# An adaLN, recurrence and FFN kernel on one Trainium2 core: the rows of six projection blocks turned by transposing DMAs instead of TensorE

## What is computed

```
x  = x + attn(cond(x, cond_512))          # first half
#   cond: modulated 512x512 product, demodulated and clipped
#   attn: h = rmsnorm; gates, a linear recurrence over the tokens;
#         hs2 = out * gate + residual
#         h2 = rmsnorm(hs2); p = (h2 @ fc) * gelu(h2 @ gate)   # 1536 wide
#         result = p @ out_w.T + out_b + hs2                  # the projection
x  = x + ffn(cond2(x, ids, states))       # second half
#   cond2: layer norms with gathered gains, a 3072 -> 512 -> 512 network
#   ffn: int8 quantisation by rows, a 512x512 product, scales
```

## Time and profile before

| what | us |
|---|---|
| median of 3 runs | 1764.82 |
| lowest and highest | 1763.02, 1766.92 |
| the profiled execution, its own time | 1766.26 |
| span of the profile | 1764.4 |
| TensorE (PE) busy | 1744.7 |
| its weight loads (PEld, beside PE) | 1419.6 |
| VectorE (DVE) busy | 1184.4 |
| ScalarE (ACT) busy | 892.9 |
| GpSimd (POOL) busy | 786.7 |

### The profile page before, as it was taken

How to read it: one execution, slowest core, us unless ns; L and a number is a source line. 1 busy time by engine, 2 the same in 40 slices (tenths; PEclk the granted TensorE clock), 3 DMA queues, 4 the chain that set the end, 5 groups by cost and what they waited for, 6 DMA issues and landing times.

```text
span 1764.4 us, 23639 instructions
## 1 busy us (share of the span) xinstructions
PE 1744.7 (99%) x8047; PEld 1419.6 (80%) x8047; DVE 1184.4 (67%) x1753; ACT 892.9 (51%) x1329; POOL 786.7 (45%) x702
## 2 busy tenths in 40 slices
PE   9999999999899999999999999999999999999998
PEld 7888888888788888888888888776887888888886
DVE  8756667569989687795563344437976577577555
ACT  7655555555676575764652222334554443544533
POOL 1111221122766656674550000016577877778742
PEclk9999999999999999999999999999999999999999
DMA  6011110120343233233536666985645444534401
GB/s 206 1 48 48 48 48 0 48 72 24 120 133 129 101 122 138 96 105 122 192 105 220 196 233 215 337 284 181 226 135 172 146 138 148 164 124 151 148 23 61
DMA packets 105800, 229.72 MB, mean 130 GB/s; under 512 B 9906, under 2 KB 10162, under 8 KB 105700
## 3 DMA queue, kind: packets, MB, share of 16 engines
q1 hardware_dynamic: 75540, 152.97, 25.3%
q0 software_dynamic: 11776, 41.95, 7.1%
q10 hardware_dynamic: 18384, 33.56, 5.7%
HBM read 169.73 MB, written 58.72 MB: 129 GB/s over the span
## 4 chain that ended last, share of the span: by engine, by line
PE 87%; DVE 5%; DMA 2%; issue 2%; ACT 1%; SPq 1%; POOL 1%; DVEq 0%; ACTq 0%
PE bank L1058 25%; PE bank L348 17%; PE bank L2025 13%; PE bank L1121 12%; PE bank L2049 5%; PE bank L2070 5%; PE bank L328 4%; PE bank L1991 2%; PE bank L2000 2%; DMA x1T_d<-x_columns 1%; SPq L1918 1%; DMA x_columns<-xT 1%; POOL u L613 1%; PE bank L1131 1%; DVE h_parts L1470 1%
## 5 line engine op out<-in xcount | busy, mean ns | idle before, releaser
L1058 PE MATMUL bank<-h_parts,mlp_w 128*128 128x512 f32 x2016 | 460.1, 389 | 4.5 <-DVE mlp_w L1474 2.4
L1058 PEld LDWEIGHTS bank<-h_parts,mlp_w 128*128 128x128 f32 x2016 | 378.0, 188 | 85.3 <-DVE mlp_w L1474 2.8
L348 PE MATMUL bank<-h_parts,gate_w 128*128 128x512 f32 x1536 | 351.1, 389 | 0.6 <-DVE h_parts L681 0.6
L348 PEld LDWEIGHTS bank<-h_parts,gate_w 128*128 128x128 f32 x1536 | 288.2, 188 | 61.8 <-issue 0.9
L2025 PE MATMUL bank<-operand_parts,int_w 128*128 128x512 f32 x1152 | 281.8, 394 | 0.4 <-DVE x_columns L1572 0.4
L1121 PE MATMUL bank<-p_parts,mlp_out_w 128*128 128x512 f32 x1152 | 275.2, 396 | 6.1 <-DVE p_parts L1484 6.1
L1121 PEld LDWEIGHTS bank<-p_parts,mlp_out_w 128*128 128x128 f32 x1152 | 215.1, 189 | 56.5 <-issue 11.8
L2025 PEld LDWEIGHTS bank<-operand_parts,int_w 128*128 128x128 f32 x1152 | 213.1, 188 | 44.4 <-PE bank L1121 0.8
L1390 POOL TENSOR_TENSOR product_out<-product_out,gelu 128x512 f32<-128x512 f32 x72 | 125.3, 1761 | 97.4 <-DVE product_out L1542 96.8
L608 POOL TENSOR_TENSOR decay_sq<-decay 128x512 f32<-128x512 f32 x32 | 39.2, 1226 | 278.8 <-DVE decay L694 278.8
L1270 ACT ACTIVATE product_copy<-bank,vec_sb 128x512 f32<-128x512 f32 x144 | 99.0, 688 | 106.7 <-PE bank L1058 105.8
(11 more groups left out here) (308 smaller groups left out, 2809.0 us busy)
## 6 DMA issues: line engine op xcount, KB each, us to landing
p_d<-product_out SPq DMA_DIRECT2D x96, 256.0 KB, 2.0
p_tile<-p_d ACTq DMA_DIRECT2D x96, 256.0 KB, 4.8
raw_mlp_w<-mlp_gate_g SPq DMA_DIRECT2D x21, 512.0 KB, 3.6
raw_mlp_w<-mlp_fc_g SPq DMA_DIRECT2D x21, 512.0 KB, 4.4
xin<-xT SPq DMA_DIRECT2D x8, 1024.0 KB
hs_d<-u SPq DMA_DIRECT2D x8, 1024.0 KB, 5.0
hs_pair<-hs_d SPq DMA_DIRECT2D x8, 1024.0 KB, 7.7
x_columns<-xT SPq DMA_DIRECT2D x8, 1024.0 KB, 6.8
```

The costliest lines, as they stand in the source:

```text
L348: i = pe.matmul(bank[:], gw[:, w, s, k, m * P:(m + 1) * P], hr[:, q, t, k, :], start=k == 0 and n == 0, stop=k == KT - 1 and n == 2)
L1058: i = pe.matmul(bank[:], wb[g % 2][:, s, w, kk, :], hop[u % 2][o][:, t, kk, :], start=first and kk == 0 and n == 0, stop=kk == 1 and n == ...
```

## The change

The rows of blocks 0 to 5 (`TURNED` = 6) are no longer made on TensorE. Since the DMA's transposition handles elements of 16 bits, transposed x1 in DRAM is looked at as halves of floats, 512 channels by 1024 halves for a block. SP's new function `turn(b)`, in body b+1, does this:

1. It waits for the store of the rows of the block before and issues one transposing DMA of 1 MB from DRAM into `x1_turned`. A partition then holds either low or high halves, since neighbouring columns become neighbouring partitions.
2. It waits for that DMA, and for the joins of the block before, and issues four DMAs, the splits, inside SBUF. Each takes every second partition of a group of turned columns and writes 64 partitions of `x1_halves`, in runs of 1 KB, so that low and high halves of a token lie on one partition.

ACT joins the halves with two copies of 16-bit elements for each quarter of the block (`join_halves`), in its tiles 8 to 11; together they write the row buffer, each every second element. The first join of a body waits for all four splits. `turn` stands in SP's program behind the load of x columns and behind the ten DMAs of body 5, and ahead of the store of the rows. SP no longer waits for transpositions before it loads x columns in those bodies, and TensorE no longer waits for the evacuation at a block's first tile. The rows of blocks 6 and 7 are made as before. The row buffer of the first six blocks moves to the place of `x1_turned`, which it overwrites.

```diff
@@ mlp_half @@
-    rows_of = [at("x1_rows", [P, TT, D], HF_AT)] * (NB - 2) + [at("x1_rows_late", [P, TT, D], G2)]
+    rows_of = [at("x1_rows", [P, TT, D], TURN_AT)] * TURNED + [at("x1_rows_late", [P, TT, D], G2)]
+    turned = at("x1_turned", [P, 2 * TT, D], TURN_AT, U16)
+    halves = at("x1_halves", [P, TT, 2, D], HF_AT, U16)
...
+    JOIN_ACT = {8: 0, 9: 1, 10: 2, 11: 3}
@@ sync_program @@
+        def turn(b):
+            sp.wait_ge(t_stored, 16 * b)
+            sp.dma_start(turned[:], x1T_halves[:, 2 * BT * b:2 * BT * (b + 1)], transpose=True).then_inc(turn_done, 16)
+            sp.wait_ge(turn_done, 16 * (b + 1))
+            sp.wait_ge(t_evac, TT * b)
+            for odd in range(2):
+                for h in range(2):
+                    sp.dma_start(halves[64 * odd:64 * odd + 64, :, h, :], turned[h:P:2, odd:2 * TT:2, :]).then_inc(halves_there, 16)
...
                 sp.wait_ge(x_stored, 16 * b)
-                sp.wait_ge(t_ps, TT * b)
+                if b - 1 >= TURNED:
+                    sp.wait_ge(t_ps, TT * (b - TURNED))
             sp.dma_start(xt[:], xT[:, :, bass.ts(b, BT)]).then_inc(x_loaded, 16)
             if b == LAST_FIRST:
                 last_w1()
                 last_w2()
                 last_c_rows()
+            if b and b - 1 < TURNED:
+                turn(b - 1)
             if b:
                 sp.wait_ge(t_evac, TT * b)
                 sp.dma_start(x1_d[:, bass.ds(TT * (b - 1), TT), :], rows_of[b - 1][:]).then_inc(t_stored, 16)
@@ tensor_program @@
                         pe.wait_ge(r1, KT * (b - 2) + c + 1)
-                        pe.wait_ge(t_evac, TT * (b - 1))
...
-                if b and j in TOK_PE:
+                if b - 1 >= TURNED and j in TOK_PE:
                     to_tokens(b - 1, TOK_PE[j])
@@ scalar_program @@
+        def join_halves(b, t):
+            act.wait_ge(halves_there, 64 * (b + 1))
+            row = rows_of[b][:, t, :].bitcast(U16).rearrange("p (d h) -> p d h", h=2)
+            act.activation(row[:, :, 0], halves[:, t, 0, :], ACT.Copy)
+            act.activation(row[:, :, 1], halves[:, t, 1, :], ACT.Copy).then_inc(t_evac, 1)
...
+                if b and b - 1 < TURNED and j in JOIN_ACT:
+                    join_halves(b - 1, JOIN_ACT[j])
-                if b and j in TOK_ACT:
+                if b - 1 >= TURNED and j in TOK_ACT:
                     evacuate_rows(b - 1, TOK_ACT[j])
```

More of the change, by code:

```diff
@@ L8 @@
 I32 = mybir.dt.int32
+U16 = mybir.dt.uint16
 ALU = mybir.AluOpType
@@ L52 @@
 HALF = 8 * KB
+TURN_AT, TURNED = 72 * KB, NB - 2
 A_AT = tuple(KB * n for n in (104, 120, 128, 96, 152, 80, 88))
@@ L95, in adaln_attn_ffn_kernel @@
     x1_d = nc.dram_tensor("x1_d", (TOK, D), F32, kind="Internal").ap().rearrange("(n p) c -> p n c", p=P)
-    x1T_d = nc.dram_tensor("x1T_d", (D, TOK), F32, kind="Internal").ap().rearrange("(k p) t -> p k t", p=P)
+    x1T_rows = nc.dram_tensor("x1T_d", (D, TOK), F32, kind="Internal").ap()
+    x1T_d, x1T_halves = x1T_rows.rearrange("(k p) t -> p k t", p=P), x1T_rows.bitcast(U16)
     ctx = ExitStack()
@@ L117, in following @@
         def following(sems, marks):
-            return mlp_half(nc, at, sems, marks, ps, vec, v, ident, ones_r, eps6, ins, xT, hs2_d, x1_d, x1T_d, p_d, out_v)
+            return mlp_half(nc, at, sems, marks, ps, vec, v, ident, ones_r, eps6, ins, xT, hs2_d, x1_d, x1T_d, x1T_halves, p_d, out_v)
         with nc.Block() as block:
@@ L822, in _, with mlp_half @@
             run()
-def mlp_half(nc, at, sems, att, ps, vec, v, ident, ones_r, eps6, ins, xT, hs2_d, x1_d, x1T_d, p_d, out_v):
+def mlp_half(nc, at, sems, att, ps, vec, v, ident, ones_r, eps6, ins, xT, hs2_d, x1_d, x1T_d, x1T_halves, p_d, out_v):
     spent = list(sems)
@@ L886, in mlp_half @@
     p_high, p_low, o_ps = sem("p_high"), sem("p_low"), sem("mlp_out_ps")
+    turn_done, halves_there = sem("x1_turn_done"), sem("x1_halves_there")
     t_ps, t_evac, t_stored = sem("x1_tok_ps"), sem("x1_tok_evac"), sem("x1_tok_stored")
@@ L1314, in group @@
                 gelu_of(g, 1)
+        def join_halves(b, t):
[3 more added lines that the diff above has]
+            act.activation(row[:, :, 1], halves[:, t, 1, :], ACT.Copy).then_inc(t_evac, 1)
         def evacuate_rows(b, t):
-            act.wait_ge(t_ps, TT * b + t + 1)
+            act.wait_ge(t_ps, TT * (b - TURNED) + t + 1)
             act.wait_ge(t_stored, 16 * b)
@@ L2231, in last_rows_out @@
             for t in ts:
-                act.wait_ge(mlp["tokens"], LAST_ROWS + t + 1)
+                act.wait_ge(mlp["tokens"], TT * (NB - 1 - TURNED) + t + 1)
                 act.activation(last_rows[:, t, :], ring[2 + t % 2][:], ACT.Copy).then_inc(mlp["tok_evac"], 1)
```

## The result

The changed kernel takes **1863.73 us**, the median of 4 runs (1856.53 to 1866.83); the kernel before took 1765.59 us beside it (4 runs, 1763.02 to 1766.92). The ratio is 1.0552 [1.0528, 1.0577]: 5.5% slower, some 98 us. The profiled execution took 1863.38 us, its span 1861.6 us, with a mean granted clock of 0.970.

The account below looks back on a forecast made before the run. TensorE, busy 1744.7 of 1764.4 us, was taken as the bound. Blocks 1 to 4 -4.5, block 5 +17.7, block 6 +3.6 us sum to +16.8 us: 1782 us against the median 1764.82; range 1768 to 1826 us.

Parts of the forecast that it names:

- What goes: Bodies 1 to 6: 96 of 112 TensorE transpositions go, 11.0 us or 0.6% of the run, all on the path.
- The joins: ACT's 48 joins replace 24 evacuations, 0.60 us each (bounds 0.3 and 1.2), hidden unless ACT is held up.
- The deadline s+22.0: Bodies 1 to 6: halves due 22.0 us after the block's first TensorE tile starts (s); each later us idles TensorE.
- Blocks 1 to 4: Halves there at s+22.7, 0.7 us late; less 1.8 us of transpositions, -1.1 us a block, -4.5 us in all.
- the nearest row moves as many bytes from the same place in the order: Blocks 1 to 4: transposing DMA priced like the store of rows, 9.5 us; bounds 2.0 and 16.8 us.
- The DMA engines are only 0.63 busy in block 1: Argument for the covered rival: DMA engines might take the transposing DMA ahead of loads queued before it.
- the covered case: Rival: waits are covered, decided in block 5; 1759 us, or 1754 us if nothing is late; chance 12%.
- Block 5: Transposing DMA issued at s+21.6 behind SP's queue, splits at s+39.5, TensorE idle 17.5 us; net +17.7 us.
- Block 6 and 7: Block 6: x1 stored at s+18, TensorE waits 7.4 us, net +3.6 us; block 7: late int_W loads cost nothing.
- The clock: Block 5 after the idle: slow matmuls, partly at 1.2 GHz, overlapping DVE work; 3 us taken for both.
- The transposing DMA is slow everywhere: Rival: 16.8 us in place of 9.5, six blocks 7.3 us later each, 44 us; 1826 us; chance 20%.
- The case beyond: Rival: DMA transposes one tile after another, an estimated 42 us a block; about 1977 us; chance 5%.

Follow-up runs that it names:

- experiment 2: Changed kernel with a plain load of the same megabyte into the same buffer in place of the transposing DMA; 1833.53 us.
- experiment 1: Changed kernel with the p_tile loads of bodies 1 to 6 cut to 16 of 512 columns; 1816.72 us.
- experiment 4: Changed kernel with the transposing DMA issued ahead of the load of x_columns; 1831.3 us.
- experiment 8: Changed kernel, four blocks instead of six, transposing DMA first, joins at tile 11 and next body's tiles 0 to 2, rows in own buffer; 1782.28 us, ratio 1.008.
- experiments 7 and 12: 7: changed kernel, rows from other data, no transposing DMA or splits, 1763.15 us; 12: kernel before, body 6's four int_W loads behind x_columns, 1777.00 us.

## Why the prediction was wrong

The step that failed is the price of the chain in blocks 1 to 4: 9.5 us for the transposing DMA, 6.6 for the splits and 4.8 for the store, where the trace has 17.7, 10.0 and 8.5 in block 3. The sign, the chain and its deadline were right; the size was not: +16.8 us forecast, 98 measured, beyond the range's 1826 us. Term by term:

- **What bounds the kernel.** Right for the kernel before: a stall of TensorE goes straight into the time. "What goes", 11.0 us all on the path, was too much: the run without them and without a substitute wins 5.1 us in the stretch and 3 in all. Here "all on the path" failed, by some 8 us: in blocks 6 and 7 the load of x columns and the store of the rows set the pace.
- **The joins.** 0.77 us each for 0.60, inside the bounds, and hidden, apart from the one pair of 1.3 us that the deadline has in it.
- **The deadline s+22.0.** Right: in block 3 the first join came 36.6 us after the store's issue, forecast 21.6, and the forecast lateness of 0.7 us plus these 15.0 is 15.7 us; the trace has 16.06.
- **Blocks 1 to 4, where the failed step weighs most.** Forecast -4.5 us, measured +53. Its terms, in block 3: the store of x1 8.5 us for 4.8, probably because the store of the rows, which left SP 17 us ahead of it before, now leaves it 7 us ahead (1044.13 and 1051.08); the transposing DMA 17.7 for 9.5; the splits 10.0 for 6.6. The sentence "the nearest row moves as many bytes from the same place in the order" priced bytes and place, and experiment 2 shows that for a plain transfer this is right to 0.1 us. It had nothing for what a transposing DMA costs beyond that: the 4100 small packets, SP's 4 to 11 us of issuing, and above all the loads on the other queue, without which it took 9.0 us (experiment 1). "I take 6.6, since their runs are shorter" looked at the wrong property: the runs cost 0.5 us, the partitions 5.3.
- **"The DMA engines are only 0.63 busy in block 1"** stood as an argument for the covered case. The change's own work on these engines was never summed; it went from 22 to 41 us a block. That sum is not a fixed one either: with the transposing DMA ahead of the load of x_columns it was 35 to 37 us (experiment 4: 0.86 to 0.88 of 41 us), and in experiment 8 it was 31 to 34.
- **Block 5.** +17.7 forecast. The queue argument held: issued at 1173.63, 19.6 us after the store of x1 (forecast 18.3), landed 11.7 us on (12.3). The idle time was 23.0 us for 17.5; the splits, 10.2 for 5.6, are most of the difference. Block 5 came to +24: this idle time and 2.9 us of slow matmuls behind the one before it, less the 1.8 us of transpositions.
- **Block 6 and 7.** +3.6 forecast, about 20 measured: idle times of 16.6 and 4.3 us. The wait is 9.2 us longer than the forecast 7.4: x1 was stored 6.5 us later than forecast, behind the last stage's loads (s+24.5 for s+18; issued at 1215.82, landed at 1233.63), the transposing DMA was 0.9 us cheaper (8.6 for 9.5) and the splits 3.6 us dearer (10.2 for 6.6). "Block 7: nothing" missed the wait behind the store of rows that experiments 7 and 12 show.
- **The clock.** I charged slow restarts once, in block 5. Each of seven stalls had one, about 2 us, as at 1090.46; in blocks 1 to 4 that alone gives back the 1.8 us of transpositions.
- **The rivals.** "The transposing DMA is slow everywhere" is the nearest to what happened, though not everywhere: in blocks 5 and 6 it took 11.7 and 8.6 us. That its ceiling of 16.8 us, the full queue's plain megabyte, meets the 17.0 of blocks 1 to 4 is luck, since in experiment 2 a plain megabyte takes 9.4 us there. The splits, the store and the clock came on top: 1826 became 1864. The case beyond, 42 us a block by the figure of the Trainium skill (VectorE: DVE Perf Modes, The three transpose paths) for one tile, did not occur; 6.5 us a megabyte in a quiet queue is some 0.2 us for each of its 32 tiles. The rule of the Trainium skill (Advanced Engine Details and Errata, X-Bar Transpose (TRN2)) that transposing DMAs are as fast as plain ones comes near in blocks 5 and 6, with 11.7 against 11.3 us and 8.6 against 7.5; beside the loads of `p_tile` in blocks 1 to 4 it does not hold, with 17.0 against 9.4 us.

What stays open: why the two neighbours of the transposing DMA cost 10.5 us together and 3.8 apart. That they share engines which are 0.96 busy is shown; the mechanism isn't. Nor is it shown what the engines could take at most. It was not tried to put the joins, and so the store of the rows, earlier in the body, nor to let the last stage read the rows as separate halves, which would need no splits.

## What to carry to other kernels

Before work is moved from a full engine to an idle-looking one, sum what it adds to that one too, in its own currency: for the DMA engines packets, partitions reached and time at the measured rate, not bytes. A chain of dependent transfers with a deadline pays every neighbour's queueing once per link, so price each link beside what really runs there, and put the bound above the nearest row where the kind of transfer is new. And measure the ceiling first: the run that drops the work and puts no transfer in its place won 3 us, so even a substitute that was free in time would have won little in this order of the program.

## What the runs showed of the hardware

- A transposing DMA of 16-bit elements, 1 MB from DRAM, lands after 6.5 us in a quiet queue and holds the issuing queue for 4.1 us, where a plain one of the same bytes holds it 0.5 us. Behind one load its issue takes 6.6 us (experiment 1), with the loads of `p_tile` beside it 9.3 to 11.5, and all that stands behind it on SP waits.
- Two neighbours of a transposing DMA can cost far more together than apart: 1.3 us beside the loads of `p_tile`, 2.5 behind the load of x_columns, 10.5 with both.
- Copies within the SBUF of one megabyte: 4.3 us over 128 partitions in runs of 2 KB, 4.8 in runs of 1 KB, 6.9 between blocks of 64 neighbouring partitions, 10.1 from every second partition, and the last is the same in a quiet queue: 101 GB/s at a DMA share of 0.92.
- A DMA share of 0.9 and more can go with 100 to 150 GB/s or with 400; low GB/s alone do not show that the engines are idle.
- ScalarE's copy of 512 uint16 elements to every second place takes 0.77 us, 0.17 more than its evacuation of 512 f32 from PSUM.
